# Mixture of experts in a one-core language-model layer: 64 fixed first tiles, a table for the rest, and a weight ring of 16 places

## The reference, cut to what matters

```
T, D, E, K, DFF = 3072, 128, 64, 2, 512
h = layernorm(x).reshape(T, D)
logits = (h @ Wr) @ codebook.T / 0.7           # one score per expert
vals, idx = top_k(softmax(logits), 2)          # every token goes to 2 of 64 experts
eh  = silu(einsum('td,edf->tef', h, W1) + b1)  # W1: 64 x 128 x 512
eo  = einsum('tef,efd->ted', eh, W2) + b2      # W2: 64 x 512 x 128
moe = sum over the token's two experts of weight * eo
shared = (silu(h @ Ws1 + bs1) @ Ws2 + bs2) * 0.25
out = x + (moe + shared) + ffn(layernorm(moe + shared))
```

## Time and profile before

| what | value |
|---|---|
| median of 3 runs | 1179.35 us (1177.79 to 1180.16) |
| the profiled execution, its own time | 1169.94 us |
| its span, first to last instruction | 1168.1 us |
| PE, DVE, ACT, POOL busy, share of the span | 75%, 61%, 57%, 34% |
| TensorE's mean granted clock, share of full | 0.909 |
| HBM read and written | 64.17 MB and 11.03 MB |

### The profile page before, as it was taken

The page is one execution under the profiler, slowest core; times in us unless marked ns, Lnnn a source line. Parts: engine busy times, 40 slices in busy tenths (PEclk is TensorE's granted clock), DMA queues, the critical chain, the costliest instruction groups (busy, mean ns, idle before and its releaser), DMA issues.

```text
span 1168.1 us, 24664 instructions
## 1 busy us (share of the span) xinstructions
PE 872.7 (75%) x7427; PEld 665.8 (57%) x7427; DVE 708.7 (61%) x2209; ACT 667.8 (57%) x1643; POOL 392.2 (34%) x458
## 2 busy tenths in 40 slices
PE   3457889789778978987898887167766666665887
PEld 1235566556555655655665565166656656665787
DVE  4398878988898898889889643311211112123776
ACT  3266878777777877777787554033433434342343
POOL 7500111322331232233123333365655555551111
PEclk9978899999999999999998888578998998897999
DMA  8200000000000000000000000447766675665000
GB/s 196 29 1 1 1 8 2 8 8 0 7 7 7 0 7 7 0 7 7 7 0 8 8 8 8 90 131 212 210 183 193 182 196 169 179 185 112 14 17 21
DMA packets 53976, 71.08 MB, mean 61 GB/s; under 512 B 10818, under 2 KB 40624, under 8 KB 53936
## 3 DMA queue, kind: packets, MB, share of 16 engines
q1 hardware_dynamic: 45456, 62.56, 19.7%
q0 software_dynamic: 8480, 8.01, 3.0%
HBM read 64.17 MB, written 11.03 MB: 64 GB/s over the span
## 4 chain that ended last, share of the span: by engine, by line
PE 36%; issue 25%; DVE 19%; DMA 8%; another core or an unknown queue 5%; POOL 3%; SPq 2%; ACT 1%; DVEq 0%; POOLq 0%
PE b_s L1207 6%; DMA b2buf<-in_L_ffn_b 5%; PE big L1334 5%; PE b_o L1374 5%; DVE tbuf L794 5%; PE big L1486 4%; PE big L1324 4%; DVE spread L794 4%; POOL pr L424 2%; DVE pr L921 2%; PE b_qk L1501 2%; PE b_s L1501 2%; PE big L1361 1%; SPq L343 1%
## 5 line engine op out<-in xcount | busy, mean ns | idle before, releaser
L1486 PE MATMUL big<-hbT,wbuf 128*128 128x128 f32 x672 | 108.5, 312 | 91.7 <-DMA b2buf<-in_L_ffn_b 47.4
L794 DVE TENSOR_TENSOR tbuf<-qT,b_qk 128x2304 f32<-128x2304 f32 x64 | 162.7, 2547 | 19.6 <-remote 10.7
L657 ACT ACTIVATE act_h<-big,wbuf 128x128 f32<-128x128 f32 x336 | 95.7, 368 | 122.5 <-PE big L1486 75.7
L541 ACT ACTIVATE tbuf<-tbuf 128x2304 f32<-128x2304 f32 x64 | 135.6, 2119 | 46.6 <-DVE tbuf L794 38.4
L1486 PEld LDWEIGHTS big<-hbT,wbuf 128*128 128x128 f32 x672 | 94.0, 216 | 103.8 <-issue 50.7
L1207 PE MATMUL b_s<-tbuf,apad 128*32 128x192 f32 x1536 | 97.5, 393 | 59.4 <-ACT p L550 51.8
L1092 DVE TENSOR_SCALAR hbT<-b_t,cols 128x128 f32<-128x128 f32 x84 | 34.3, 409 | 147.8 <-PE b_t L1479 85.1
L482 POOL DMA_INDIRECT hrow<-tok_dram,igather x84 | 85.5, 1018 | 80.9 <-PE b_t L1479 37.4
L491 POOL DMA_INDIRECT eo_dram<-eo,iscatter x84 | 85.9, 1023 | 56.7 <-issue 32.7
L424 POOL TENSOR_TENSOR pr<-pr,rs 96x384 f32<-96x384 f32 x64 | 52.7, 824 | 149.5 <-DVE rs L928 149.5
L1207 PEld LDWEIGHTS b_s<-tbuf,apad 128*32 128x32 f32 x1536 | 51.0, 126 | 90.4 <-issue 48.8
(11 more groups left out here) (209 smaller groups left out, 1916.0 us busy)
## 6 DMA issues: line engine op xcount, KB each, us to landing
wbuf<-in_wpack SPq DMA_DIRECT2D x84, 514.0 KB
b2buf<-in_L_ffn_b SPq DMA_DIRECT2D x84, 64.0 KB
tok_dram<-tn SPq DMA_DIRECT2D x32, 96.0 KB
spread<-eo_dram SPq DMA_DIRECT2D x1, 2688.0 KB, 16.0
out<-of SPq DMA_DIRECT2D x16, 96.0 KB, 1.7
hrow<-tok_dram,igather POOLq DMA_INDIRECT x84
eo_dram<-eo,iscatter POOLq DMA_INDIRECT x84
tab_dram<-tid_now,slot_now POOLq DMA_INDIRECT x64
```

Of the source, the lines that this page charges most:

```text
L541: act.activation(v, v, ACT.Tanh).then_inc(s["tanh"], 1)
L657: last = act.activation(act_h[:, r % 2, c * TILE:(c + 1) * TILE], big[r % 2][:, c * TILE:(c + 1) * TILE], ACT.Silu, bias=wbuf[:, r, 2 * DF ...
L794: dve.tensor_tensor(ring[c % TRING].rearrange("p (x m n) -> p x m n", m=CQ, n=N), qv.unsqueeze(3).to_broadcast([D, SPLIT * QG, CQ, N]), kv ...
L1486: last = pe.matmul(big[r % 2][:, c * TILE:(c + 1) * TILE], wbuf[:, r, c * D:(c + 1) * D], hbT[:, r % 2, :], start=True, stop=True)
```

## The change

**Fixed first tiles.** Tiles 0 to 63 are now tiles of experts 0 to 63, written out one after the other in the code of every engine: expert e's first 128 assignments. The slot becomes `rank * 64 + expert`, so that the numbers of all 64 first tiles are the first 128 rows of the table. SP loads the table straight into SBUF as columns in two transfers (`ids_first`, then `ids_rest`), after the last write of it has landed; POOL's gathers and scatters of the fixed tiles take their column there. `ttab` lists only tiles for assignments past an expert's 128th; they follow in the loop over turns, at least three of them. For these, ACT reads the position of the column out of `ttab` into a register, once for `igather` and once for `iscatter`.

**Weights.** b2 is laid into the packed weights by the host, so that one transfer of 578 KB brings W1, W2, b1 and b2. The buffer has 16 places for the fixed tiles; the tiles of the loop use the first 4 of them. The first 16 experts are loaded before the stage begins: 12 to 15 at the start, 8 to 11 after the attention weights that lie there are used up, 0 to 7 between the token stores of the last four pairs (after a wait for the last score of the additive attention, whose ring lies in those places).

**Small things.** The last scatters no longer wait for one another; ACT copies `iscatter` after silu and not before; the table's initial values come from the buffer `vv`, whose first write waits for that transfer.

```diff
-TABN = E * T
+SLOTS = 16
+STATIC = E // RING
+MAXO = -(-(T * TOPK // TILE) // RING) * RING
+LEAST = 3
+HB = T // TILE + 1
+TABN = E * HB * TILE
-WCOLS = 2 * DFF + FC
+WCOLS = 2 * DFF + FC + D
...
@block.sync
+            for e in range(clear, SLOTS):
+                load_expert(e, e)
+            sp.wait_ge(s["raw_ev"], 4)
+            for e in range(early, clear):
+                load_expert(e, e)
...
-            with sp.Fori(1, PAIRS) as p:
+            with sp.Fori(1, PAIRS - 4) as p:
                 store_tokens(p)
-
+            sp.wait_ge(s["score"], CH * PAIRS)
+            for p in range(PAIRS - 4, PAIRS):
+                for e in range((p - PAIRS + 4) * early // 4, (p - PAIRS + 5) * early // 4):
+                    load_expert(e, e)
+                store_tokens(p)
+            sp.wait_ge(s["scat"], 16 * TOPK * B)
+            table = tab_dram.rearrange("(j p e) a -> p j (e a)", p=TILE, e=E)
+            cells = ids.rearrange("p (j e) -> p j e", e=E)
+            load(cells[:, 0:1, :], table[:, 0:1, :], s["ids_first"])
+            load(cells[:, 1:HB, :], table[:, 1:HB, :], s["ids_rest"])
+            for e in range(SLOTS, E):
+                sp.wait_ge(s["eo"], e - SLOTS + 1)
+                load_expert(e, e)
-            def load_tile(u, r, again=True):
-                t = u * RING + r
-                if again:
-                    gate(sp, s["eo"], t - RING + 1)
-                e = sp.value_load(ttab[0:1, bass.ds(t, 1)], min_val=0, max_val=E - 1)
-                sp.dma_start(wbuf[:, r, :], io["wpack"][bass.ds(e, 1), :, :]).then_inc(s_w[r], 16)
-                sp.dma_start(b2buf[:, r, :], io["L0_ffn_b2"][bass.ds(e, 1), :].rearrange("a d -> (a d)")
-                             .partition_broadcast(TILE)).then_inc(s_w[r], 16)
+            def load_more(u, r):
+                if known(u):
+                    sp.wait_ge(s["eo"], E - SLOTS + r + 1)
+                else:
+                    gate(sp, s["eo"], (u + (STATIC - 1)) * RING + r + 1)
+                e = sp.value_load(ttab[0:1, bass.ds(u * RING + r, 1)], min_val=0, max_val=E - 1)
+                load_expert((u, r), e)
...
@block.gpsimd
-            pool.indirect_dma_start(
-                idrows[:, :], None, tab_dram.rearrange("(a b) n -> a (b n)", b=TILE), ...
+            pool.wait_ge(s["ids_first"], 16)
+            for t in range(E):
+                gather_tile(t)
+                if t >= 6:
+                    scatter_tile(t - 6)
...
-                if r == 1:
-                    gate(pool, s_st[2], 16 * last)
-                    gate(pool, s_st[3], 16 * last)
-                if r:
-                    gate(pool, s_st[r - 1], 16 * (last + 1))
-                scatter_tile(last, r)
+                scatter_tile((last, r))
...
@block.scalar
+            def cell(u, r):
+                at = act.value_load(ttab[0:1, bass.ds(u * RING + r + MAXO, 1)], min_val=0, max_val=HB * E - 1)
+                return ids[:, bass.ds(at, 1)]
+            for t in range(E - RING):
+                silu(t)
...
             with act.Fori(1, turns - 1) as u:
                 for r in range(RING):
                     gather_index(u + 1, r)
+                    silu((u, r))
                     scatter_index(u, r)
-                    silu(u, r)
...
@block.tensor
+            for t in range(E):
+                expert1(t)
+                tile_turn(t + 1 if t < E - 1 else (0, 0))
+                if t:
+                    expert2(t - 1)
```

More of the change, by code:

```diff
@@ L223, in program @@
         eo = [sb(f"eo{r}", [TILE, D]) for r in range(RING)]
[L226 to L231, removed]
+        ring = [arena[:, i * CW:(i + 1) * CW] for i in range(TRING)]
+        er = arena[0:N, 0:PAIRS * G * TOPK * D].rearrange("p (a g k d) -> p a g k d", a=PAIRS, g=G, k=TOPK)
         wl = sb("wl", [N, G * TOPK])
@@ L259, in program @@
             *[f"{m}_{n}" for m in ("var", "rstd") for n in ("x1", "x2", "h0", "h1")],
-            "cnt", "tinfo", "trow", "ttab", "idrows", "idf", "ids_t", "iall", "cg", "cs",
-            *[f"{n}{r}" for n in ("w", "h", "st") for r in range(RING)],
+            "cnt", "tinfo", "trow", "ttab", "ids_first", "ids_rest", "cg", "cs",
+            *[f"w{i}" for i in range(SLOTS)], *[f"{n}{r}" for n in ("h", "st") for r in range(RING)],
             "tr", "hbT", "g1", "silu", "g2", "eo",
@@ new lines, in _ @@
+            with pool.Fori(2, turns) as u:
+                for r in range(RING):
+                    gather_tile((u, r))
+                    if r < 2:
+                        scatter_tile((u - 2, r + 2))
+                    else:
+                        scatter_tile((u - 1, r - 2))
+            before, last = turns_less(pool, 2), turns_less(pool, 1)
+            scatter_tile((before, 2))
+            scatter_tile((before, 3))
+            for r in range(RING):
+                scatter_tile((last, r))
@@ L576, in vv_copy @@
             def vv_copy(p, k):
+                if known(p) and p == 0:
+                    act.wait_ge(s["tab_init"], 16)
                 act.wait_ge(s["hv"], 4 * p + k + 1)
@@ L650, in _ @@
+            for t in range(E - RING):
+                silu(t)
             act.wait_ge(s["ttab"], 1)
+            act.wait_ge(s["ids_rest"], 16)
             turns = turns_less(act, 0)
-            def silu(u, r, after=True):
-                t = u * RING + r
-                act.wait_ge(s["g1"], t + 1)
-                for c in range(FC):
-                    last = act.activation(act_h[:, r % 2, c * TILE:(c + 1) * TILE],
-                                          big[r % 2][:, c * TILE:(c + 1) * TILE], ACT.Silu,
-                                          bias=wbuf[:, r, 2 * DFF + c:2 * DFF + c + 1])
-                last.then_inc(s["silu"], 1)
```

342 lines of the change are left out of this document (166 added, 176 removed).

## The result

The changed kernel takes 1193.57 us (median of 4 runs, 1191.25 to 1194.93) against 1179.76 for the kernel before on the same chip (4 runs, 1177.79 to 1182.27): ratio 1.0121, 95% interval 1.0090 to 1.0153. The forecast was 1159 us, at most 1186. The profiled execution took 1192.94, 23.0 more than that of before, with a span of 1191.1 (before 1168.1).

A forecast was written before the change was run, and what follows sets the result against it. Waits, above all for weights, paced the expert stage; POOL would pace the fixed tiles. 1169.94 - 8.8 (stage) - 7.5 (start) - 4.5 (end) = 1149.1 us profiled; 20.8 off the median gives 1159 us, range 1138 to 1186.

The forecast's parts named there:

- The tiles, counted first: Expert stage: 100 tiles run where 84 did; the 16 more cost 56 us at 3.48 us each.
- The fixed tiles: First 64 expert tiles: POOL's gather and scatter set 2.65 us a tile, 170 us in all, bounds 162 to 185.
- What disturbs the ring, 0.83 us: Old weight loop: 0.83 of 3.48 us a tile put down to SP's lateness, ACT behind a scatter, and TensorE's clock.
- The loop of 7.96 us: Old kernel's weight ring: product, result, load and next product take 7.96 us in three tiles, 2.65 us a tile.
- Weights: Fixed tiles: a 592 kB load takes 1.5 us at 394 GB/s, so weights keep up with POOL's 2.65 us.
- The loop: Tiles past the 128th assignment: 3.15 us each with ACT's two register reads, 35 steps, 110 us, bounds 93 and 122.
- The start: Start of the expert stage: first gather at 751.8 instead of 759.28, 7.5 us earlier.
- the rival on it: Start of the expert stage: `ids_rest` blocks the first gathers, 7.5 us lost, 1166 us; 6 in 100.
- The moved loads, costed at nothing: First 16 experts' weight loads, moved before the expert stage: no cost; without cover up to 4 x 3 us.
- The end: End of the expert stage: last scatters without their chain, SP's load at 1057.5 instead of 1062.02, 4.5 us won.
- The rivals: Five other outcomes for the whole kernel: 1141 us (20 in 100), 1174 (12), 1166 (6), 1200 (14), 1179 (5).
- The one on the other side: Loop tiles: ACT's two register reads set the pace, 4.3 us a tile, 42 us more, 1200 us; 14 in 100.

The follow-up runs named there:

- e3: Changed kernel with fixed tiles only for the 46 experts with tokens and two empty ones, 84 tiles instead of 100; ratio to before 0.9706.
- e4: Changed kernel with eight places instead of four for gathered rows and results in the fixed tiles; fixed tile 3.18 us, ratio to before 1.0146.
- f2: e10 plus a second indirect gather of the same rows, which nothing reads, in each fixed tile; fixed tile 3.22 us, ratio to before 1.0171.
- e10: Changed kernel with the fixed tiles' scatters as plain transfers from SP, gathers still indirect on POOL; fixed tile 1.97 us, ratio to before 0.9473.
- e11: Changed kernel with the fixed tiles' gathers and scatters as plain transfers, still issued by POOL; fixed tile 1.94 us, ratio to before 0.9488.
- g1: Changed kernel with SP writing all tiles' results by plain transfers and 64 indirect gathers in the last stage; 1130.1 us, ratio to before 0.9625.
- e12: Changed kernel with the fixed tiles' gathers as plain transfers from SP, scatters still indirect on POOL; fixed tile 2.06 us, ratio to before 0.9532.
- f1: e10 plus an unused memset of 128 by 1024 on POOL behind each fixed tile's gather; fixed tile 2.16 us, ratio to before 0.9589.

## Why the prediction was wrong, step by step

- **The tiles, counted first:** right. 100 tiles ran, and 16 more were the larger item: e3 gives 2.9 us for each where I had put 3.48 at the old pace.
- **The fixed tiles: the step that failed.** "What is left is POOL, 2 x 1.327 = 2.65 us a tile": they took 3.16, 202.5 us instead of 170, outside the bounds of 162 to 185. POOL's four in a row are right, but a bound of one engine at its own best pace leaves out what its work does to another. Two indirect transfers in a tile hold TensorE's completions up, which the prediction put at nothing: 3.16 to 3.22 us with two, 2.50 with three in two tiles, 1.97 with one, though PE has the same products. The text asked for one more look "if the fixed tiles take over 2.9 us", at DMA landing or DVE's wait for scatters; it was neither (e4, f2).
- **What disturbs the ring, 0.83 us:** SP's lateness, ACT and the clock were named. The late completions were in the same table, 39.4 and 39.0 us of "remote", nearly as much as the 47.4 and 44.2 in the earlier trace rows. With the waits on weights and scatters gone, ACT's rose from 39.4 to 86.1 and those of DVE's `eo` from 17.0 to 44.3, in 313 us instead of 290. That the removed waits had been cover for these is my reading of it; no run tests it. The loop of 7.96 us was put together without the 4.00 us by which the result of tile 41 came late in the very rows that it was read from.
- **Weights:** right. They don't pace the fixed tiles; e10 and e11 load a tile's in 1.9 us, at 318 and 362 GB/s.
- **The loop:** 3.44 instead of 3.15, 10 us more, within its bounds. The reason given, ACT's two register reads, isn't shown. g1 took away one of them together with the scatter, and the loop fell to 2.95. What the traces do show is lateness: silu is 0.70 us late in the mean of the changed kernel's loop and never in g1's.
- **The start:** 6.3 instead of 7.5 us. The first gather came at 751.66, forecast 751.8, but from it to the first product 4.54 us pass, where it was 3.18 before. `ids_rest` is in flight then, 5.5 us from issue to landing; whether it takes the 1.4 us wasn't tried; the rival on it had put up to 7.5.
- **The moved loads, costed at nothing:** the last table write is issued 2.6 us later than in the earlier trace rows (747.04 against 744.47). 2.26 of it are there already in the pair of table writes at 309.55, at 307.29 before. What of the changed first part takes them wasn't tried. That the first gather came on time is luck: I let the last write land 3.82 us after POOL is done with it, but SP issues the load of the table at 749.12, 1.16 us after (747.96). Two errors of 2.6 us cancel.
- **The end:** 3.8 and 1.1 us, forecast 4.5: right.
- **The rivals:** none held. The one on the other side had the sign and, at 1200, nearly the time, by luck: with 4.3 us a tile it gave the loop 30 us too much, and the loss lay in the fixed tiles, which took 32.5 us more than it had for them.

Sum by the steps: +32.5 in the fixed tiles and +10.4 in the loop turn the forecast's 8.8 won in the stage into 34.1 lost, and start and end differ by 1.2 and 0.4.

## What to carry to other kernels

A wait whose releaser the profile can't name is the first to look at: set the recorded end of the producer beside the start of its consumer, and see which engine runs something without a pause in between. Before a change takes waits off an engine, ask whether the next bound has ever been seen at that pace with all the others at work; POOL's 2.65 us had been seen for four transfers only. Where each round has an indirect gather and an indirect scatter, write in the order of the work instead and collect at the end; here the last stage, in which the collecting is itself made of neighbouring gathers, gave 23 us of the gain back.

## What the hardware showed

- With two indirect transfers from POOL in each tile, TensorE's results reach the engines that wait for them up to 4.8 us after their recorded end in the changed kernel, 1.0 in the mean; with one a tile, with two plain ones, or with a memset of POOL beside one, silu starts 0.03 to 0.06 us after in all fixed tiles but one each of e12, f1 and g1. Whether the array itself is slowed or only its signals wait isn't shown: no run tells them apart.
- It isn't the rows moved: an empty expert's indices are all out of bounds, so its tile moves none, and it costs 2.9 us all the same (e3).
- It isn't the kind: a second gather (f2) does what the scatter did. How far apart two indirect transfers must be is open; in e10 they start 1.9 us apart, and in f2 and the changed kernel 1.3 us at the closest.
- The Trainium skill, in DMA: Bandwidth & Descriptors, section Issuing engine by pattern, gives simple stores to Sync and indirect ones to gpsimd. In e11 plain transfers stay on gpsimd and the kernel is as fast as with SP (0.9488 and 0.9461, intervals overlap), so the gain is not in which engine issues but in what POOL issues.
